# The placement of an edge list before a graph layer: pieces side by side, parts spread by ScalarE, turns beside the next group's products, eight pairs gathered from the placed table

## What is computed

```python
h = jnp.maximum(_layernorm(x, axis=-1), 0.0)
S = h[src]
def edge_nn(v, W, b):
    t = relu(v @ W.T + b)
    return relu(t @ W.T + b)
for r in range(2):
    msgs = where(rel == r, edge_nn(S, W_rel[r], b_rel[r]), msgs)
agg = segment_sum(msgs, dst, num_segments=n_nodes)
i, f, g, o = split(agg @ W_ih.T + b_ih + b_hh, 4)
c = sigmoid(i) * tanh(g)
hn = sigmoid(o) * tanh(c)
out = x + MLP(hn)        # two relu layers of 128, then 256 outputs
```

## Time and profile before

| | us |
|---|---|
| median of three runs | 2260.63 |
| lowest, highest | 2260.33, 2261.53 |
| the profiled execution | 2269.79 |
| its span, first to last instruction | 2268.1 |
| mean granted TensorE clock of it | 0.959 |

### The profile page before, as it was taken

How to read it: one execution, slowest core, us unless ns; L and a number is a source line. 1 busy time by engine, 2 the same in 40 slices (tenths; PEclk the granted TensorE clock), 3 DMA queues, 4 the chain that set the end, 5 groups by cost and what they waited for, 6 DMA issues and landing times.

```text
span 2268.1 us, 51837 instructions
## 1 busy us (share of the span) xinstructions
PE 2080.7 (92%) x14224; PEld 1405.7 (62%) x14225; DVE 1755.9 (77%) x4311; ACT 1627.2 (72%) x3364; POOL 1187.8 (52%) x917
## 2 busy tenths in 40 slices
PE   5858767767999999999999999999999999999996
PEld 4746555555666666666666666666666666445553
DVE  8537555555888888888888888888888887788886
ACT  2437655555888888888888888888888887666663
POOL 0036777777766665666666666666666644100000
PEclk7559999898999999999999999999999999999998
DMA  9954555557789898889888988888888988988886
GB/s 383 425 207 93 95 95 100 98 97 141 135 174 185 170 180 174 179 170 175 175 178 173 178 177 180 178 178 183 170 178 175 180 153 162 193 188 191 190 188 156
DMA packets 400606, 396.90 MB, mean 175 GB/s; under 512 B 263738, under 2 KB 343158, under 8 KB 394360
## 3 DMA queue, kind: packets, MB, share of 16 engines
q0 software_dynamic: 91200, 157.34, 40.8%
q1 hardware_dynamic: 306788, 238.12, 40.0%
q10 hardware_dynamic: 2516, 0.14, 0.1%
HBM read 185.88 MB, written 156.97 MB: 151 GB/s over the span
## 4 chain that ended last, share of the span: by engine, by line
PE 78%; issue 7%; POOL 5%; ACT 3%; DMA 3%; DVE 3%; another core or an unknown queue 1%; POOLq 0%; DVEq 0%; ACTq 0%; SPq 0%
PE bank L1469 33%; PE bank L1435 9%; PE bank L1416 9%; PE bank L1483 6%; PE bank L1508 5%; PE bank L1452 4%; PE bank L1398 3%; PE bank L1492 3%; POOL agg L664 2%; POOL xg L648 2%; DMA agg<-summed,scatter_idx 2%; PE bank L1308 2%; PE bank L1409 2%; PE bank L1427 1%; DMA a_lo<-row_lo 1%
## 5 line engine op out<-in xcount | busy, mean ns | idle before, releaser
L664 POOL DMA_INDIRECT agg<-summed,scatter_idx x400 | 665.5, 1664 | 501.4 <-ACT summed L724 261.4
L1469 PE MATMUL bank<-a_hi,ihT 128*128 128x512 f16 x2400 | 714.0, 379 | 2.4 <-DMA a_lo<-row_lo 2.2
L648 POOL DMA_INDIRECT xg<-in_x,src_ring x400 | 426.1, 1065 | 271.0 <-DMA src_ring<-src_slot 138.1
L1469 PE MATMUL bank<-a_lo,ihT 128*128 128x512 f16 x1200 | 454.8, 379 | 0.0
L1469 PEld LDWEIGHTS bank<-a_hi,ihT 128*128 128x128 f16 x2400 | 234.4, 98 | 213.0 <-issue 2.3
L1435 PE MATMUL bank<-relT,h_hi 128*128 x1600 | 321.5, 275 | 0.0
L1416 PE MATMUL bank<-s_hi,relT 128*128 128x256 f16 x1600 | 292.9, 278 | 0.0
L672 POOL DMA_DIRECT2D y<-in_x x100 | 133.4, 1334 | 298.0 <-DVE y L1202 287.6
L1077 DVE SCALAR_TENSOR_TENSOR h_lo<-bank,h_hi 128x512 f16<-128x512 f32 x200 | 137.5, 688 | 120.4 <-ACT h_hi L751 114.6
L757 ACT ACTIVATE xn<-xg,shift,rstd 128x256 f32<-128x256 f32 x400 | 216.4, 591 | 10.3 <-DVE shift L1111 10.3
L1070 DVE SCALAR_TENSOR_TENSOR s_lo<-bank,s_hi 128x512 f16<-128x512 f32 x200 | 136.4, 682 | 111.2 <-ACT s_hi L730 73.4
(11 more groups left out here) (197 smaller groups left out, 4642.4 us busy)
## 6 DMA issues: line engine op xcount, KB each, us to landing
agg_in<-agg SPq DMA_DIRECT2D x100, 512.0 KB
y<-in_x POOLq DMA_DIRECT2D x100, 512.0 KB
out<-y SPq DMA_DIRECT2D x100, 512.0 KB
agg<-zeros SPq DMA_DIRECT2D x24, 2112.0 KB, 15.8
dst_ring<-dst_rows SPq DMA_DIRECT2D x200, 128.0 KB
xg<-in_x,src_ring POOLq DMA_INDIRECT x400
agg<-summed,scatter_idx POOLq DMA_INDIRECT x400
src_ring<-src_slot SPq DMA_DIRECT2D x200, 1.0 KB
```

The source lines that it names most:

```text
L648: nc.gpsimd.indirect_dma_start(out=xg[:, k.slot(8), t, :], out_offset=None, in_=x[:, :], in_offset=bass.IndirectOffsetOnAxis(ap=src_ring[: ...
L664: nc.gpsimd.indirect_dma_start(out=agg[:, :], out_offset=bass.IndirectOffsetOnAxis(ap=scatter_idx[:, k.slot(8), t:t + 1], axis=0), in_=sum ...
L1469: last = nc.tensor.matmul(N_C[c % 2][:, 0:UNIT], lhs, rhs, start=i == 0, stop=i == len(todo) - 1)
```

## The change

1. The layout of iota_win, hot_win and win_parts is turned: columns outermost, then parts, windows innermost, so that the 48 values of a column lie side by side.
2. The multiplication takes the parts from parts_beside, in which ScalarE has repeated each part 16 times (`spread_parts`, three copies for a group, for groups 1 to 3). For group 0 it reads parts16 with the repeat in the access pattern.
3. TensorE does the turns of group i - 1 one or two a batch beside the products of group i, and the pieces of group i - 2 there too; there are two more rounds in place of one. The tile numbers are loaded in portions, just ahead of the pieces that need them (0 or 1 a batch). ScalarE's and VectorE's orders follow: windows(i + 1) come after the eighth batch of lanes, tiles(i - 1) after the fifth.
4. The first eight pairs are gathered with indices straight from src_slot; SyncE's loads of src_ring start with pair 8.

```diff
-            nc.scalar.copy(iota_win[:, :, :], iotaf[0:ROWS, 0:WINDOWS].unsqueeze(2).to_broadcast([ROWS, WINDOWS, GROUP]))
+            nc.scalar.copy(iota_win[:, :, :], iotaf[0:ROWS, 0:WINDOWS].unsqueeze(1).to_broadcast([ROWS, GROUP, WINDOWS]))
...
-                if k.within(PAIRS):
-
-                    wait_from(sp, gathered[k.slot(8)], k.turn(8) * 32)
+                if k.within(PAIRS) and not (isinstance(k.n, int) and k.n < 8):
+
+                    if not isinstance(k.n, int) or k.n >= 16:
+                        sp.wait_ge(gathered[k.slot(8)], k.turn(8) * 32)
...
-                    pool.wait_ge(src_loaded[k.slot(8)], 16 * (k.turn(8) + 1))
+                    if isinstance(k.n, int) and k.n < 8:
+                        pool.wait_ge(src_slots_ready, 1)
+                        rows = src_slot[:, 2 * k.n:2 * k.n + 2]
+                    else:
+                        pool.wait_ge(src_loaded[k.slot(8)], 16 * k.turn(8))
+                        rows = src_ring[:, k.slot(8), :]
...
-            for i in range(COL_GROUPS):
+            def spread_parts(i, n):
+                act.wait_ge(parts_ready, 1)
+
+                act.wait_ge(win_ready, i)
+                nc.scalar.copy(parts_beside[:, :, n, :],
+                               parts16[:, n, i * GROUP:(i + 1) * GROUP].unsqueeze(2).to_broadcast([ROWS, GROUP, WINDOWS])
+                               ).then_inc(parts_beside_ready, 1)
+
+            for i in range(COL_GROUPS + 1):
                 for b in range(BATCHES):
-                    cols_copy(i * BATCHES + b)
-                for g in range(TURNS):
-                    turn_copy(i, g)
+                    if i < COL_GROUPS:
+                        cols_copy(i * BATCHES + b)
+                    if i + 1 < COL_GROUPS and b < PARTS:
+                        spread_parts(i + 1, b)
+                    if i:
+                        for g in range(b * TURNS // BATCHES, (b + 1) * TURNS // BATCHES):
+                            turn_copy(i - 1, g)
...
-                                                win16[:, cols].unsqueeze(1).to_broadcast([ROWS, WINDOWS, GROUP]),
+                                                win16[:, cols].unsqueeze(2).to_broadcast([ROWS, GROUP, WINDOWS]),
...
-                nc.vector.tensor_tensor(win_parts[:, i % 2, :, :, :],
-                                                hot_win[:, :, :].unsqueeze(1).to_broadcast([ROWS, PARTS, WINDOWS, GROUP]),
-                                                parts16[:, :, cols].unsqueeze(2).to_broadcast([ROWS, PARTS, WINDOWS, GROUP]),
-                                                ALU.mult).then_inc(win_ready, 1)
+                all_parts = [ROWS, GROUP, PARTS, WINDOWS]
+                if i == 0:
+                    parts = parts16[:, :, cols].rearrange("p n c -> p c n").unsqueeze(3).to_broadcast(all_parts)
+                else:
+                    dve.wait_ge(parts_beside_ready, i * PARTS)
+                    parts = parts_beside[:, :, :, :]
+                nc.vector.tensor_tensor(win_parts[:, i % 2, :, :, :], hot_win[:, :, :].unsqueeze(2).to_broadcast(all_parts),
+                                        parts, ALU.mult).then_inc(win_ready, 1)
...
-            for i in range(1, COL_GROUPS + 1):
-                if i < COL_GROUPS:
-                    windows(i)
-                tiles(i - 1)
-                if i < COL_GROUPS:
-                    for b in range(BATCHES):
-                        lanes(i * BATCHES + b)
+                if b == 7:
+                    windows(1)
+            for i in range(1, COL_GROUPS):
+                for b in range(BATCHES):
+                    lanes(i * BATCHES + b)
+                    if b == 4:
+                        tiles(i - 1)
+                    if b == 7 and i + 1 < COL_GROUPS:
+                        windows(i + 1)
+            tiles(COL_GROUPS - 1)
...
-                                            win_parts[:, i % 2, :, :, b * BATCH + c].rearrange("p n w -> p (n w)"),
+                                            win_parts[:, i % 2, b * BATCH + c, :, :].rearrange("p n w -> p (n w)"),
...
-            for i in range(COL_GROUPS + 1):
-                if i:
-                    _, at_tile = nc.values_load_multi_w_load_instructions(
-                        first_tile[0:1, i - 1, :], engines=[mybir.EngineType.PE], min_val=0, max_val=TILES - 1)
+            for i in range(COL_GROUPS + 2):
+                if i == 1:
+                    pe.wait_ge(sums_read, 1)
+                    pe.wait_ge(first_ready, 1)
+                at_tile = []
                 for b in range(BATCHES):
                     if i < COL_GROUPS:
                         columns(i * BATCHES + b)
-                    if i:
-                        piece(i - 1, b, at_tile)
-                if i < COL_GROUPS:
-                    if i == 0:
-                        pe.wait_ge(sums_read, 1)
-                        pe.wait_ge(first_ready, 1)
-                    for g in range(TURNS):
-                        turn(i, g)
+                    if i >= 2:
+                        at_tile += first_tiles(i - 2, len(at_tile), ((b + 1) * WINDOWS // BATCHES + 1) // 2)
+                    if 1 <= i <= COL_GROUPS:
+                        for g in turns_beside(b):
+                            turn(i - 1, g)
+                    if i >= 2:
+                        piece(i - 2, b, at_tile)
```

More of the change, by code:

```diff
@@ L316, in build @@
         iota_lane = tmp("iota_lane", [ROWS, P, BATCH], F16)
-        iota_win = tmp("iota_win", [ROWS, WINDOWS, GROUP], F16)
+        iota_win = tmp("iota_win", [ROWS, GROUP, WINDOWS], F16)
         iota_span = tmp("iota_span", [GROUP, SPAN], F16)
         hot_lane = tmp("hot_lane", [ROWS, HOT_SLOTS, P, BATCH], F16)
-        hot_win = tmp("hot_win", [ROWS, WINDOWS, GROUP], F16)
-        win_parts = tmp("win_parts", [ROWS, 2, PARTS, WINDOWS, GROUP], F16)
+        hot_win = tmp("hot_win", [ROWS, GROUP, WINDOWS], F16)
+        parts_beside = tmp("parts_beside", [ROWS, GROUP, PARTS, WINDOWS], F16)
+        win_parts = tmp("win_parts", [ROWS, 2, GROUP, PARTS, WINDOWS], F16)
         col_parts = tmp("col_parts", [P, 2, WV, GROUP], F16)
@@ L392, in build @@
         iotas_ready = sem("iotas_ready")
+        parts_ready = sem("parts_ready")
+        parts_beside_ready = sem("parts_beside_ready")
         win_ready = sem("win_ready")
@@ L649, in step @@
                             out=xg[:, k.slot(8), t, :], out_offset=None, in_=x[:, :],
-                            in_offset=bass.IndirectOffsetOnAxis(ap=src_ring[:, k.slot(8), t:t + 1], axis=0)
+                            in_offset=bass.IndirectOffsetOnAxis(ap=rows[:, t:t + 1], axis=0)
                         ).then_inc(gathered[k.slot(8)], 16)
@@ L950, in _ @@
             nc.vector.tensor_copy(lane16[:, :], lane_i[:, :])
-            chained(nc.vector.tensor_copy(parts16[:, :, :], parts_i[:, :, :]))
+            nc.vector.tensor_copy(parts16[:, :, :], parts_i[:, :, :]).then_inc(parts_ready, 1)
+            dve.wait_ge(parts_ready, 1)
             dve.wait_ge(iotas_ready, 1)
@@ L1320, in turn, with first_tiles, turns_beside @@
                 last.then_inc(turn_done, 1)
+            def first_tiles(i, lo, hi):
+                if lo == hi:
+                    return []
+                _, values = nc.values_load_multi_w_load_instructions(
+                    first_tile[0:1, i, lo:hi], engines=[mybir.EngineType.PE], min_val=0, max_val=TILES - 1)
+                return list(values)
+            def turns_beside(b):
+                return range(b * TURNS // BATCHES, (b + 1) * TURNS // BATCHES)
             def clear(start):
```

## The result

The changed kernel takes 2246.48 us (median of 4 runs, 2245.49 to 2246.82) where the kernel before takes 2261.08 (2260.33 to 2265.3): ratio 0.9931, 95% interval [0.9914, 0.9948]. It is 14.6 us faster; 12.7 had been forecast (2247.9). The two profiled executions are further apart than that: 2269.79 before, 2245.49 after, 24.3 us. In the profile the step that was to move as a block did not: scatter 0 comes 22.6 us earlier (163.29 for 185.87 in the timelines of GpSimd), the clear of the placement 13.6. So the number was near, and the profile says that something behind it was not as the prediction told it. All ratios leave out two executions, one of the kernel before (2784.56 us) and one of the layout alone (6146.94 us).

A forecast was written before the change was run, and what follows sets the result against it. The placement, a chain of waits nearly all on TensorE, was taken to set the pace; its parts summed to a clear at 122.6 instead of 135.31, 12.7 us earlier, so 2260.63 - 12.7 = 2247.9 us, range 2236 to 2258.

The forecast's parts named there:

- First product: Placement, group 0: VectorE's repeated operand runs at the fp32 rate, so the first product moves from 34.52 to 37.9 us.
- Pairs of products: Placement, TensorE: with columns side by side a pair takes 60 ns instead of 93; ends 40 and 93.
- What the pairs are worth: Placement: clear 12.7 us earlier with 60 ns pairs, 5.9 with 93; rival that stride is no cause: 2254.7, chance 0.17.
- Groups: Placement, groups 0 to 3: 13.5, 17.0, 17.3 and 16.3 us, turns lying beside the next group's products.
- Register loads: TensorE's tile numbers: 0.65 us each, mostly hidden; last stretches 11.4 and 9.2 us; rival slower kernel, 2277.6, chance 0.06.
- The direct gathers, costed at nothing: Behind the placement: first gather 2.8 us earlier against the placed table, counted as nothing because VectorE's weight work covers it.
- the late end of the zeroing: Behind the placement: gathers start at about 126 us while zeroing fills DMA till about 133; costed nothing, 3 us for range.
- the placement sets nothing: Rival on the whole placement: time stays at 2260.6; no chance of its own, within the 0.04 for the rest.
- ScalarE's stall: Wait from 157.29 to 169.99 us, taken as unchanged against the placed table; earlier or gone 0.18, worse 0.10.
- ends with the gathers: Rival on ScalarE's wait: it comes 2.8 us earlier, 2245.1; shares the 0.18 for earlier or gone.
- is a matter of ScalarE's program: Rival on ScalarE's wait: it may vanish, 10.5 us earlier (within 0.18), or fall worse, up to 10 later (0.10).
- The block: Everything after the placement moves forward with the clear, 12.7 us; scatter 0 moving by another amount would mean failure.

The follow-up runs named there:

- the schedule alone: Kernel before with turns beside the next group's products, VectorE's new order and tile numbers in portions; old layout, no spreads, no direct gathers: ratio 0.9992.
- after's second profile: Profile of the changed kernel run once more, unedited, on a chip where the kernel before takes 2269.8 us: 2253.99 us, ratio 0.9922.

## Why the prediction was right, and where it was not

**First product.** 37.9 forecast, 37.70 measured. A repeated innermost element costs the fp32 rate: right. The Trainium skill's report ("Vector Engine (DVE) Microarchitecture Reference", 5.1) agrees.

**Pairs of products.** 60 ns forecast, 58 to 59 measured; the layout alone isolates the stride. Right.

**What the pairs are worth.** Wrong. Between a 60 ns and a 93 ns placement the prediction counted 6.8 us, with the late first product in both, so the layout as a whole was to bring 3.4. The step that failed is the length of the groups with 93 ns pairs: 70.9 us, or 67.6 in the same terms for the schedule alone (which has no spreads and no slower hot_win). That kernel took 63.6 (first product 34.4, last 98.0), against 60.6 with the new layout (37.7 to 98.3), and the 3.0 us that the groups gain are spent by a first product that comes 3.3 us later. Group by group it is 12.9, 14.6, 18.3 and 17.8 us against 13.4, 15.1, 17.7 and 14.4. Groups 0 and 1 wait for VectorE, and there a shorter pair buys nothing; group 3 carries the gain, where TensorE binds, and the higher clock has a part in it.

**Groups.** 64.1 us forecast for the four, 60.6 measured: 13.4, 15.1, 17.7 and 14.4 for 13.5, 17.0, 17.3 and 16.3. In group 1 the engine that binds is not ScalarE, as the prediction had it, but VectorE (15.12 of 15.15 us busy from 51.10 to 66.25); ScalarE did its 25 copies, counted at 16.5, in 14.81. Group 3 had the higher clock (0.77 on average from 82 to 107 us), which the prediction allowed for at 2 to 4 us but did not count.

**Register loads.** 0.65 us of sequencer time each was forecast, from the shortest load in the trace (306 ns). A load of first_tile takes 568, so 0.74 with its register operation, and the two stretches without products take 23.4 us (98.3 to 121.69) for the 20.6 forecast. The error of the groups and this one cancel to 0.9 us in the clear. Taking sixteen of the loads out of these stretches brought the clear forward by 7.4 us, the higher clock that came with it included.

**The direct gathers, costed at nothing.** This is the step that failed most. Taken alone in the kernel before they are worth 2.5 us; but the sum moved the placement by 12.7 us and did not ask what SP's eleven ring loads would then stand behind. They stand behind the zeroing (15.5 us from issue to gather), so that without direct gathers the change brings nothing (ratio 1.0000) and with them all of it. The prediction had named the late end of the zeroing as a risk for the gathers' packets (3 us, and 1.1 of it came: the statistics moved 12.5 us for 13.6), and passed over the queue that the indices came through. The rival "the placement sets nothing", which is what the change does without the direct gathers, had no chance of its own, only a share in the 0.04 for the rest, with the argument that the chain runs through it without a gap; a chain doesn't show what would be next if it were shorter.

**ScalarE's stall.** It was assumed to keep its length, and the rivals "ends with the gathers" and "is a matter of ScalarE's program" stood beside it. The first is the right one: it ended 4.6 us after the start of the last gather of an unbroken run in the kernel before (165.41, 170.01), 4.5 in after's second profile, and 2.9 to 4.7 in every other that had it, at the first h_hi, the third, or an m_hi. The argument against its being occasional (three runs within 1.2 us) did not hold: those runs lasted 9 us less than the profiled execution, which should have said that they were not like it. Where both kernels have the stall, the direct gathers and the placement move the run of gathers forward as a whole and the stall with it: 15.9 us (2269.89 to 2253.99) for the 12.7 forecast. In the result, where after shows no stall, it is 14.6, and how the kernel before got to its 2261.08 there is not shown.

**The block.** Right from scatter 0 on: 15.7 us earlier (185.70 to 169.99) for 15.9 us of time in after's second profile; 22.6 and 24.3 between the two profiles first shown. Not right from the clear to scatter 0: the prediction named it as a sign of failure if the two move by different amounts, and they did, 13.6 and 22.6 us in the first pair of profiles, 14.2 and 15.7 in the second.

**Luck.** The forecast of 12.7 us came near because the change happened to hold the part that the sum put at nothing: with it the gain is 15.9 us (2269.89 to 2253.99), without it 0.5 (2269.83 to 2269.29), no change that can be told. And the clear at 121.69 for 122.6 is a group sum too long by 3.5 us and two last stretches too short by 2.8.

**Two readings.** The prediction has TensorE busy about 80% of a window from 30 us on; that holds from 57 us (20.27 of 25), while from 30 to 57 it was 16.48 of 27. And dst_rows goes out behind three ring loads, not two (eleven less eight). Neither changes the sum.

**Open.** What ScalarE and TensorE wait for in a run of gathers. The profile names no queue. The Trainium skill ("Runtime: NRT & Kernel Launch", Instruction fetch mechanics) says that each engine's sequencer fetches its next page of instructions through a DMA queue of its own; a fetch that the gathers hold up would be one reading. The records speak against it: the profile lists the packets of two instruction queues (56 and 46 packets in the kernel before), and neither queue has a packet in any of the eleven stalls, nor is one let through at a stall's end. In the kernel before, none starts between 134.0 and 179.7 us; from 157 to 170 us there are only these (packets, MB, share of 16 engines):

```profile
q0 software_dynamic: 452, 1.22, 32.2%
q1 hardware_dynamic: 375, 0.12, 5.5%
```

Open too is how the kernel before spends its time on a chip where it takes 2260.8 us: no profile of it there was taken.

## What to carry to other kernels

Before costing an earlier finish, list what the freed step triggers and read for each the queue that it goes through, and what will be in that queue at the new moment; two edits that are worth next to nothing alone (0.9992, and 0.9986 or 2.5 us) were worth 0.6% together. A small load of indices does not belong behind bulk transfers on one queue. And measure each part alone and left out: the part that was meant to carry the gain, the layout, carried none of it that could be measured.

## What the runs showed of the hardware

- Runs of eight to twenty indirect gathers issued by GpSimd every 1.25 us hold ScalarE (it stood idle for 5.1 us behind the run of eight and for up to 14.4 behind twenty, some 2 of them for TensorE's product), and slow TensorE to one matmul in 1.4 us (seen in one profile); pauses of 1.9 us after every second gather take that away. On three chips it is there in every profile with such a run; in the first profile of after a run of 22 gathers did no harm. What is waited for is open.
- A 1 KB load issued behind zeroing transfers of 2112 KB on SP's queue took 15.5 us, some 3 of them (135 to 138.3 us) behind a single DMA engine that was later than the other fifteen; on GpSimd's queue a gather issued into the same traffic (117.1) was there when VectorE asked for it, 9.5 us later.
- Moving operands read 200 bytes apart cost 93 ns for 48 columns at the lower clock level; side by side it is 58, at the lower level and at the upper.
- One value loaded into a TensorE register takes 568 ns, eight at once 1118 to 1311.
